# Routing weights carried in the rows, layer 3's residual added by the experts, and a last stage that only normalises

## The reference, cut to what matters

```python
def _moe(x, router_w, w1, b1, w2, b2):                       # layer 0
    logits = jnp.einsum('bsd,de->bse', x, router_w)
    top_logits, indices = jax.lax.top_k(logits, K)           # K = 2, E = 8
    weights = jax.nn.softmax(top_logits, axis=-1)
    h = jax.nn.gelu(jnp.einsum('bsd,edf->ebsf', x, w1) + b1[:, None, None, :])
    stacked = jnp.einsum('ebsf,efd->ebsd', h, w2) + b2[:, None, None, :]
    ...
    return jnp.einsum('bskf,bsk->bsf', selected, weights)
...
tokens = x.reshape(-1, D_MODEL)                              # layer 3
capacity = _capacity(s, N_EXPERTS)                           # 320 rows for each of 16 experts
gate_logits = tokens.astype(jnp.float32) @ gate_w.T
combine_weights, sec_mask = _top1_router(gate_logits, capacity)
dispatch = jnp.einsum('sec,sd->ecd', sec_mask.astype(tokens.dtype), tokens)
h = jax.nn.gelu(jnp.einsum('ecd,edf->ecf', dispatch, w1))
expert_out = jnp.einsum('ecf,efd->ecd', h, w2)
out = jnp.einsum('sec,ecd->sd', combine_weights.astype(tokens.dtype), expert_out)
```

## Time and profile before

| | |
|---|---|
| median of 3 runs | 1375.3 us (1372.81 to 1380.28) |
| the profiled execution | 1378.92 us |
| its span, first to last instruction | 1377.1 us |
| granted TensorE clock, mean over the span | 0.886 of full speed |
| PE, DVE, ACT, POOL busy | 79%, 61%, 47%, 27% of the span |

### The profile page before, as it was taken

One profiled execution on the slowest core, in us unless ns is written; L12 is line 12 of the kernel. 1 busy time (PEld: TensorE's weight loads), 2 busy tenths in 40 slices (PEclk: granted clock), 3 DMA queues, 4 the chain that ended last, 5 costly groups with the idle time before them and its releaser, 6 DMA issues.

```text
span 1377.1 us, 33088 instructions
## 1 busy us (share of the span) xinstructions
PE 1092.7 (79%) x9623; PEld 736.5 (53%) x9623; DVE 841.7 (61%) x3277; ACT 644.4 (47%) x1505; POOL 375.2 (27%) x602
## 2 busy tenths in 40 slices
PE   5989999885499993777779989999876889729940
PEld 2334444433488883676645545555565778616720
DVE  3789999985233335975646666667446677742237
ACT  2577777763344441554326656666534433204410
POOL 4012333235344454332200000000022033333553
PEclk9999999997699996999968999999999655559975
DMA  5223332212566676210032222221011011034513
GB/s 160 75 72 82 87 89 81 77 34 85 156 204 203 206 215 212 81 35 31 25 85 61 61 61 55 62 61 29 19 35 39 16 43 43 30 111 120 168 60 93
DMA packets 146575, 119.23 MB, mean 87 GB/s; under 512 B 16658, under 2 KB 134675, under 8 KB 146323
## 3 DMA queue, kind: packets, MB, share of 16 engines
q1 hardware_dynamic: 136912, 100.73, 25.6%
q0 software_dynamic: 7168, 14.37, 3.1%
q10 hardware_dynamic: 2370, 2.56, 0.7%
HBM read 47.26 MB, written 23.41 MB: 51 GB/s over the span
## 4 chain that ended last, share of the span: by engine, by line
PE 53%; DVE 20%; issue 11%; POOL 7%; ACT 4%; DMA 3%; SPq 1%; DVEq 1%; POOLq 0%; ACTq 0%
PE po L1535 7%; PE po L475 5%; PE pm L438 5%; PE pt L1529 4%; PE pm L1529 4%; DVE xg L341 3%; POOL rstd L332 3%; PE pm L425 3%; PE p L394 3%; DVE mx L656 3%; DVE st L320 2%; PE p L537 2%; PE p L515 1%; DVE mv L323 1%; POOL sorted L1375 1%
## 5 line engine op out<-in xcount | busy, mean ns | idle before, releaser
L656 DVE TENSOR_REDUCE mx<-pm 128x2 f32<-128x512 f32 (+1 forms) x512 | 304.2, 617 | 120.2 <-PE pm L451 73.7
L600 ACT ACTIVATE ex<-pt 128x512 f32<-128x512 f32 (+1 forms) x512 | 269.1, 547 | 162.3 <-PE pt L444 85.0
L329 POOL TENSOR_SCALAR ve<-mv 128x2 f32<-128x2 f32 x96 | 22.2, 232 | 676.5 <-DVE mv L323 676.5
L438 PE MATMUL pm<-ks,qs 64*128 64x256 bf16 (+1 forms) x1024 | 172.6, 259 | 7.4 <-DVE mx L656 4.9
L444 PE MATMUL pt<-qs,ks 64*128 64x256 bf16 (+1 forms) x1024 | 164.5, 250 | 0.6 <-ACT ex L600 0.3
L1609 POOL DMA_INDIRECT result<-ye,to_row x128 | 122.7, 958 | 150.9 <-issue 107.8
L475 PE MATMUL po<-ex,va 128*32 128x256 f32 (+1 forms) x2048 | 153.3, 371 | 0.0
L438 PEld LDWEIGHTS pm<-ks,qs 64*128 64x128 bf16 x1024 | 73.9, 98 | 88.5 <-issue 51.4
L1535 PE MATMUL po<-he,we 128*128 128x256 f32 (+1 forms) x448 | 112.9, 395 | 0.6 <-DVE yt L1573 0.4
L425 PE MATMUL pm<-hide_q,half_id 64*128 64x256 bf16 (+1 forms) x512 | 88.6, 259 | 15.0 <-DVE mx L656 9.3
L1535 PEld LDWEIGHTS po<-he,we 128*128 128x128 f32 x448 | 85.0, 190 | 19.3 <-DVE yt L1573 0.6
(11 more groups left out here) (294 smaller groups left out, 2478.4 us busy)
## 6 DMA issues: line engine op xcount, KB each, us to landing
we<-in_pack SPq DMA_DIRECT2D x40, 514.5 KB, 3.8
xs<-xg SPq DMA_DIRECT2D x96, 128.0 KB, 2.0
qs<-parts SPq DMA_DIRECT2D x192, 64.0 KB, 2.0
ks<-parts SPq DMA_DIRECT2D x192, 64.0 KB, 2.0
we<-in_pack SPq DMA_DIRECT2D x16, 512.0 KB, 3.5
xe<-sorted SPq DMA_DIRECT2D x56, 132.0 KB, 2.2
yr<-result SPq DMA_DIRECT2D x48, 128.0 KB, 2.2
xr<-xg SPq DMA_DIRECT2D x32, 128.0 KB, 2.3
```

Source lines behind the costliest of these rows:

```text
L438: last_m = pe.matmul(mine[:, e * S + k0:e * S + k1], queries, keys[:, k0:k1], start=not causal, stop=e == 1 or not causal)
L600: nc.scalar.activation(ex[j % 2][:, :, :].rearrange("p (e g) k -> p g e k", g=2)[:, 1 - u, :, lo:S], pt[:, u, :].rearrange("p (b k) -> p b ...
L656: nc.vector.tensor_reduce(mx[q.slot % 2][:, qt, u, 2 * b:2 * b + 2], pm[:, u, :].rearrange("p (b k) -> p b k", k=S)[:, :, 0:hi], AX.X, ALU ...
```

## The change

1. Layer 0: the two weights go into column D+1 of the token's two rows in `xr` rather than into `weight`, and so travel with the rows. POOL's scatter waits for `wt_sb` (part 6) rather than for `place_sb` (part 5). In the experts DVE copies the weight column of `xe` to `w_row`, and multiplies the result by it as it leaves PSUM. The combining stage has no `wrow` and no weights: two tensor_tensor additions of 128 x 256 rather than four scalar_tensor_tensor of 128 x 128.
2. Layer 3: the weight goes into `rows3`, and the experts compute `ye = result * weight + row` with three scalar_tensor_tensor that read PSUM and `xe`. So `xe` is needed until then, and SP's load of group n waits for `ye_sb` of group n-4 rather than for `to_row_sb`.
3. The normed rows of the linear stage are copied to `result3` in DRAM rather than to `xg`, and the 2 MB of zeros are gone. Experts' results then overwrite the rows of their tokens.
4. The last stage: SP loads finished rows straight into `mixed.res` (`last_sync`), and DVE only normalises (`last_vector`). A load waits for the norm of the sequence four earlier. The pipeline has three DVE steps.

```diff
@@ heads_pool
-                    wait_apart(pool, place_sb, q.n + 1, passed)
+                    wait_apart(pool, wt_sb, 5 * (q.n + 1), passed)
@@ linear_sync
-                    sp.dma_start(xg[:, bass.ds(2 * q.n, 2), :], rows3[q.slot][:, :, 0:D]).then_inc(rows_moved[q.slot], 16)
+                    sp.dma_start(yd3[bass.ds(SPARE + q.n * S, S), :].rearrange("(t p) d -> p t d", p=P),
+                                 rows3[q.slot][:, :, 0:D]).then_inc(rows_moved[q.slot], 16)
@@ put, layer 0 (layer 3 likewise into rows3)
-                    nc.vector.reciprocal(weight[:, of_seq, 0:1], sm[s][:, 1, :].unsqueeze(2)).then_inc(wt_sb, 1)
+                    nc.vector.reciprocal(xr[q.slot][:, 0, :, D + 1:D + 2], sm[s][:, 1, :].unsqueeze(2)).then_inc(wt_sb, 1)
...
@@ experts_sync
-                    wait_apart(sp, to_row_sb, a + q.back(3), passed)
+                    wait_apart(sp, to_row_sb if first else ye_sb, a + q.back(3), passed)
@@ experts_vector
+                        if biased:
+                            nc.vector.tensor_copy(w_row[q.slot][0:m, i:j, :], xe[q.slot][0:m, i:j, D + 1:D + 2]
+                                                  ).then_inc(w_row_sb, 1)
...
-                    for i, j, m in whole:
-                        last = nc.vector.tensor_copy(ye[q.slot][0:m, i:j, :],
-                                                     po1[0:m, i * D:j * D].rearrange("p (t d) -> p t d", d=D))
+                    if biased:
+                        dve.wait_ge(w_row_sb, q.n + 1)
+                        last = nc.vector.tensor_tensor(ye[q.slot][:, 0:2, :],
+                                                       po1[:, 0:2 * D].rearrange("p (t d) -> p t d", d=D),
+                                                       w_row[q.slot][:, 0:2, :].to_broadcast([P, 2, D]), ALU.mult)
+                    else:
+                        for i, m in pieces(T):
+                            last = nc.vector.scalar_tensor_tensor(ye[q.slot][0:m, i:i + 1, :],
+                                                                  po1[0:m, i * D:i * D + D].unsqueeze(1),
+                                                                  xe[q.slot][0:m, i, D + 1:D + 2],
+                                                                  xe[q.slot][0:m, i:i + 1, 0:D], ALU.mult, ALU.add)
@@ experts_pool
-                pool.wait_ge(zeroed, 48)
+                for s in rows_moved:
+                    pool.wait_ge(s, 48 * (SEQS // SLOTS))
@@ combine_vector
-                if (q := at(0)):
-                    wait(dve, mixed.res_sb, a + q.back(3))
-                    nc.vector.tensor_copy(wrow[q.slot][:, :, 0:choices],
-                                          weight[:, bass.ds(2 * q.n, 2), 0:choices]).then_inc(wrow_sb, 1)
...
+                        nc.vector.tensor_tensor(part[q.slot % 2][:, :, :], yr[q.slot][:, :, 0, :], src,
+                                                ALU.add).then_inc(part_sb, 1)
...
+                    nc.vector.tensor_tensor(mixed.res[q.slot][:, :, :], yr[q.slot][:, :, choices - 1, :], src,
+                                            ALU.add).then_inc(mixed.res_sb, 1)
@@ the last stage
+        def last_sync(sp, n):
+            for s in grp_out:
+                sp.wait_ge(s, OUTS0 + OUTS3)
+            def step(at):
+                if (q := at(0)):
+                    wait_apart(sp, mixed.ln_x, 2 * (n + q.back(3)), passed)
+                    sp.dma_start(mixed.res[q.slot][:, :, :], yd3[...]).then_inc(gathered[q.slot], 16)
+                if (q := at(4)):
+                    wait_apart(sp, mixed.ln_x, 2 * (n + q.n + 1), passed)
+                    sp.dma_start(out[...], xg[:, bass.ds(2 * q.n, 2), :]).then_inc(out_done, 16)
+            sweep(sp, 5, step)
+        def last_vector(dve, n, got):
+            def step(at):
+                if (q := at(0)):
+                    wait_apart(dve, gathered[q.slot], got // SLOTS + 16 * (q.turn + 1), passed)
+                    norm_stats(dve, q, n, mixed, loaded=True)
+                if (q := at(2)):
+                    norm_apply(dve, q, n, mixed)
+            sweep(dve, 3, step)
@@ sync block
-            sp.dma_start(yd3[SPARE:SPARE + SEQS * S, :]..., zt[:, 0:2 * D]...).then_inc(zeroed, 16)
```

More of the change, by code:

```diff
@@ L312, in copy_xt, with norm_stats @@
             nc.scalar.copy(xt[q.slot][:, 1:1 + S], p0[:, 0:S]).then_inc(xt_sb, 1)
-        def norm_stats(dve, q, done, of=None, bank=None):
+        def norm_stats(dve, q, done, of=None, bank=None, loaded=False):
             of = of or every
-            dve.wait_ge(of.res_sb, done + q.n + 1)
+            if not loaded:
+                dve.wait_ge(of.res_sb, done + q.n + 1)
             for t in range(2):
@@ L779, in post_norm_stack @@
             inv1 = [sb(f"inv1_{i}", [P, 2], F32, mem) for i in range(2)]
-            wrow = [sb(f"wrow{i}", [P, 2, 2], F32, mem) for i in range(SLOTS)]
             yr = [sb(f"yr{i}", [P, 2, 2, D], F32, mem) for i in range(SLOTS)]
@@ L1302, in put @@
                     dve.wait_ge(wt_sb, w0 + 3)
-                    nc.vector.reciprocal(weight[:, of_seq, 0:1], sm[s][:, 1, :].unsqueeze(2)).then_inc(wt_sb, 1)
+                    nc.vector.reciprocal(xr[q.slot][:, 0, :, D + 1:D + 2], sm[s][:, 1, :].unsqueeze(2)).then_inc(wt_sb, 1)
                 elif part == 6:
                     dve.wait_ge(wt_sb, w0 + 4)
-                    nc.vector.tensor_tensor(weight[:, of_seq, 1:2], e2.unsqueeze(2), weight[:, of_seq, 0:1],
-                                            ALU.mult).then_inc(wt_sb, 1)
+                    nc.vector.tensor_tensor(xr[q.slot][:, 1, :, D + 1:D + 2], e2.unsqueeze(2),
+                                            xr[q.slot][:, 0, :, D + 1:D + 2], ALU.mult).then_inc(wt_sb, 1)
             else:
@@ L1333, in put @@
                     nc.vector.tensor_tensor(lost, pl[s][:, 2, :], dump[:, of_seq], ALU.subtract).then_inc(wt_sb, 1)
-                    nc.vector.tensor_tensor(weight[:, of_seq, 0:1], inv_e.unsqueeze(2), keep.unsqueeze(2),
+                    nc.vector.tensor_tensor(rows3[q.slot][:, :, D + 1:D + 2], inv_e.unsqueeze(2), keep.unsqueeze(2),
                                             ALU.mult).then_inc(wt_sb, 1)
@@ L1451, in post_norm_stack @@
         xe = [sb(f"xe{i}", [P, 4, RW]) for i in range(SLOTS)]
+        w_row = [sb(f"w_row{i}", [P, 3, 1]) for i in range(SLOTS)]
         to_row = [sb(f"to_row{i}", [P, 4], U32) for i in range(SLOTS)]
@@ L1651, in step @@
                     if choices == 2:
[L1652 to L1656, removed]
-                        src = part[q.slot % 2][:, :, :]
@@ L1658, in step @@
-                    for t in range(2):
-                        last = nc.vector.scalar_tensor_tensor(mixed.res[q.slot][:, t:t + 1, :],
-                                                              yr[q.slot][:, t, choices - 1:choices, :],
-                                                              wrow[q.slot][:, t, choices - 1:choices],
-                                                              src[:, t:t + 1, :], ALU.mult, ALU.add)
-                    last.then_inc(mixed.res_sb, 1)
+                        nc.vector.tensor_tensor(part[q.slot % 2][:, :, :], yr[q.slot][:, :, 0, :], src,
+                                                ALU.add).then_inc(part_sb, 1)
@@ L1671, in then @@
                     sp.dma_start(out[bass.ds(2 * q.n, 2)].rearrange("t p d -> p t d"),
                                  xg[:, bass.ds(2 * q.n, 2), :]).then_inc(out_done, 16)
-            combine_sync(sp, n, 1, yd3, OUTS0 + OUTS3, 7, then)
+            sweep(sp, 5, step)
             sp.wait_ge(out_done, 16 * SEQS)
+        def last_vector(dve, n, got):
[6 more added lines that the diff above has]
+            sweep(dve, 3, step)
@@ L1795, in _ @@
             experts_vector(dve, NG, CAP3, E3, False)
-            for s in rows_moved:
-                dve.wait_ge(s, 48 * (N // SLOTS))
-            combine_vector(dve, N, 1, 32 * N)
+            last_vector(dve, N, 32 * N)
         @block.gpsimd
```

17 lines of the change are left out of this document (7 added, 10 removed).

## The result

The changed kernel takes 1457.82 us (median of 5 runs, 1455.02 to 1461.74) against 1378.78 for the kernel before (5 runs beside them, 1372.81 to 1380.28). The ratio is 1.0576, 95% interval 1.0548 to 1.0603. The profiled execution of the changed kernel took 1456.86 us, its span is 1455.1 us, and its mean granted clock 0.871 (before 0.886).

The account below looks back on a forecast made before the run. PE was taken to bound layer 3's experts, DVE the combining and last stages. Against the median, 1375.3 + 77.5 (+59 + 27 - 6 - 4 + 1.5) gave 1453 us, range 1417 to 1476.

Parts of the forecast that it names:

- the small terms: Last stage, combining with layer 1 and layer 0's scatter: -6, -4 and +1.5 us, together -8.5.
- The ring: Layer 3's experts: result transposed, `ye`, load, `xe` transposed; twelve groups each start 4.93 us later, +59 us.
- The clock: Layer 3's experts: PE's clock falls in each pause, 2.25 us lost in each of twelve steps, +27 us.
- The rule of the Trainium skill: A loop of tiles that each wait for a transfer starts every tile throttled; by it the 27 us are paid.
- Layer 1's window: Earlier trace, layer 1's stage: a pause left the clock alone; by it the clock costs 0.
- the rival at 1426: Layer 3's experts: the ring holds, but the clock does not fall, or only now and then; 1426 us, chance 0.17.
- The last stage: DVE's work shrinks, but loads wait for the norm four sequences earlier; steps of 1.88 us, -6 us.
- Combining: Combining stage with layer 1's attention: two additions replace four scalar_tensor_tensor on DVE, sixteen steps, -4 us.
- The scatter: Layer 0: POOL waits 1.9 us longer for the second weight, almost fitting its idle time; +1.5 us.
- Hidden: Writing rows to `result3` costs nothing; layer 0's product and `w_row` copy on DVE are covered, else +4 us.
- The rival in which the wait is hidden: Layer 3's experts: the load is back in time, so the kernel is not slower; 1367 us, chance 0.05.
- the point of decision: Layer 3's experts: the wait is hidden if the result's transposes come at least 4.9 us before those of `xe`.

Follow-up runs that it names:

- e6_filled9: The changed kernel with 9 unused matmuls ahead of the `xe` transposes of groups 4 to 15 in layer 3's experts; 1426.69 us, ratio 1.0343.
- e5_layer0_alone: The kernel before with only layer 0's part of the change (point 1); 1377.22 us, ratio 0.9994.
- e8_scatter_wait: The kernel before with one edit: POOL's scatter in layer 0 waits for the second weight; 1380.18 us, ratio 1.0011.
- e2_aside: The changed kernel with DVE copying the rows of `xe` aside, so the load waits for `to_row` and the copy, not `ye`; 1375.79 us, ratio 0.9982.
- e7_eight: e3_reorder with eight buffers instead of four for the last stage's rows; 1364.74 us, ratio 0.9901 to the kernel before.
- e10_eight_again: e7_eight run once more, unchanged, on another chip; 1359.8 us, ratio 0.9878 to the kernel before.
- e3_reorder: The changed kernel, layer 3: PE transposes the result before the two products, DVE does `ye` before `yt`, wait kept; 1373.9 us, ratio 0.9974.
- e4_filled: The changed kernel with 17 unused matmuls ahead of the `xe` transposes in layer 3's experts, two of twelve groups left unfilled; 1460.74 us, ratio 1.0599.

## Why the prediction was right, and where its sizes were off

The forecast was 1453 us in a range of 1417 to 1476, and 1457.8 came out. 3.5 of the 4.8 us between them are the median of before, 1378.8 with more runs for the 1375.3 that I started from. The difference was 79.0 us for a forecast of 77.5. The mechanism was right, but that the sum came so close is luck: by the spans the pauses cost 7.8 us less than forecast, and the small terms, from which 8.5 us of gain were expected, brought only 2.7 (4.75 in the last stage, less the later start of 2.05). The drain of the experts added 1.85 and the clock 0.5.

- **The ring** (+59, ends 55 to 61): right in kind and place, too large, and just below its own lower end of 55. The pauses of the twelve groups are 3.97 and 47.28 us, 51 in all. They last 3.95 to 4.71 us each, and only three of the twelve reach the 4.4 that the prediction gave as the least. Three durations were mis-sized, all taken from work beside the ring. `ye` starts 0.75 after the transposes of the result (1265.57 to 1266.32), not 0.84 as in the earlier trace rows; it takes 0.85 us and not 1.08, since one of the three has half the rows and the median of all is 334 ns; and from the second issue to PE it is 2.28, not the 2.49 of the earlier trace rows. Together 0.53 us: 4.93 becomes 4.40 by start times in this step; by idle time of PE the mean is 4.27. The issues (0.27, 0.58) were exact.
- **The clock** (+27, ends 0 and 63): it fell with every one of the pauses (mean 0.80 from 1234 to 1407), and its cost is 78.80 - 51.25 = 27.5 us in the steps and most of the 1.85 in the drain. The 4.5 us at half speed, taken from the stage's beginning in the earlier trace rows, were a little short for some steps and long for others: it is 2.5 a step by PE's busy time for 2.25 forecast. The rule of the Trainium skill that the prediction weighed (TensorE: Matmul & The Clock Gate, HAM oscillation — how this bites in real kernels) agrees with the trace: behind each of the twelve pauses the first product, `pt`, takes 2.50 us, its length at the lower level, where it takes 1.34 at the upper. Layer 1's window with 0.76 us of work in 2.00, which spoke for the rival at 1426, is not a case of the same kind. PE's longest standstill in it is 1.25 us, up to 606.12. `e6_filled9` is what that rival's world would look like, and it measured 1426.69.
- **The last stage** (-6, ends -10 and -3): -4.75. The ring of load and norm is there, in pairs of steps; W + L is 3.96, not 3.76, because both are a little longer: 1.43 and 2.47 in the pair read above, for 1.36 and 2.4.
- **Combining** (-4) measured -3.1 from its start to its end. **The scatter** (+1.5): layer 0's experts begin 1.0 us later and the combining 1.7, which is within what these starts differ by among the traces that have this part of the change. `e5_layer0_alone` finds both terms together at nothing that can be told, and `e8_scatter_wait` the second alone also. The -2.5 that the prediction has for the two lies within the interval of `e5_layer0_alone`; so does 0.
- **Hidden**: the fill of `result3`, `w_row` and the product on DVE show no loss; `e2_aside`, which has them all, is at 0.9982. The start of layer 3's experts is 2.05 us later, but that start moves by 5 us between two executions of one kernel (1234.11 in `e7_eight`, 1228.87 in `e10_eight_again`).

The rival in which the wait is hidden needed the result's transposes 4.9 us ahead of those of `xe`. `e3_reorder` puts them 4.7 us ahead, a little short of that, and the loss is gone but for two short waits: the point of decision was right, and the order on PE is what decided it.

## What to carry to other kernels

When a consumer further down the pipeline comes to read a buffer, ask which instruction now frees it, and what stands on that engine between the freeing and the next use of the slot. Here the number of slots stayed four, yet the last instruction of one step freed what the first of the next needed, and a transfer of 2.3 us that had been hidden became, with `ye` and the issues before it, a pause of 4.3 us, with some 5 us of work at half clock behind it. A copy aside (0.48 us on an engine with time to spare) or another order on PE takes it away. A loss of clock is part of a pause's price: here it added half as much again.

A stage in which the work becomes shorter than the round trip of its buffers gains only until that ring binds. Here the step of the last stage takes 1.21 us with eight buffers and 1.98 with four.

## What I had not expected

- The clock stands at 1.00 through most of the idle time and falls about when PE restarts: in the pause before 1270.30 it was at 1.00 throughout, in the unfilled one of `e4_filled` at a mean of 0.90. Whoever looks for the fall inside the pause finds little of it; it is paid for in the work after.
- Matmuls that nothing uses kept the clock at 1.00 over 108 us, and made the kernel faster by 31 us, although the rows came no sooner in the ring. In this kernel the pause was cheaper filled than empty.
- An fp32 matmul of 128 x 256 is recorded as two that start 0.22 us apart.
- DVE lost 5.2 us of 60.6 in a stage that it bounds. The stage became 3.1 us shorter, and that is too little to be seen in the time of the whole kernel (0.9994, interval 0.9972 to 1.0015).
- In the drain of layer 3's experts it is POOL's queue of scatters, 3.7 us a group, that sets the end. A step of PE that is 0.28 us shorter gained almost nothing, since it left one result more to that queue.
